# Banded attention: far products that read queries and keys in the tokens' order, with a step of 16 elements

## The reference, cut to what matters

```
OFFSETS = 0..32, 48, 64, 96, 128, 192, 256, 384        # 16 heads of 16 elements
scores[n, delta] = q[n] . k[n - delta] * scale + pos_bias[delta, head]   # -inf where n < delta
out[n] = sum over delta of softmax(scores)[n, delta] * v[n - delta]
x = x + (out * sigmoid(gate)) @ Wout + bout
```

## Time and profile before

| | |
|---|---|
| three runs | 3300.21, 3304.84 and 3306.57 us; median 3304.84 |
| the profiled execution | 3302.18 us; span from first to last instruction 3300.4 us |
| mean granted clock of the span | 0.918 |
| PE, DVE, ACT, POOL busy | 2711.5, 1657.7, 1460.1, 877.2 us |
| banded attention | from the start to about 1330 us |

### The profile page before, as it was taken

How to read it: one execution, slowest core, us unless ns; L and a number is a source line. 1 busy time by engine, 2 the same in 40 slices (tenths; PEclk the granted TensorE clock), 3 DMA queues, 4 the chain that set the end, 5 groups by cost and what they waited for, 6 DMA issues and landing times. The chain is left out here.

```text
span 3300.4 us, 102182 instructions
## 1 busy us (share of the span) xinstructions
PE 2711.5 (82%) x46240; PEld 1581.4 (48%) x46240; DVE 1657.7 (50%) x2797; ACT 1460.1 (44%) x1537; POOL 877.2 (27%) x561
## 2 busy tenths in 40 slices
PE   2678787878787887698669989898989898997897
PEld 1455565656555655443334444444444444443443
DVE  3455444444444444520656666666666666664501
ACT  1344444444444453342225555555555554555522
POOL 3343434343435242000322222222212121211002
PEclk8789888889897988799779999999999999999998
DMA  8333323232433332459132222222212222220498
GB/s 198 81 99 75 96 68 99 66 99 72 105 79 98 75 99 50 124 241 421 61 90 59 59 59 59 59 59 56 61 41 60 50 60 55 59 50 5 173 419 327
DMA packets 232618, 343.72 MB, mean 104 GB/s; under 512 B 113396, under 2 KB 141240, under 8 KB 215800
## 3 DMA queue, kind: packets, MB, share of 16 engines
q1 hardware_dynamic: 206952, 309.35, 32.2%
q10 hardware_dynamic: 25232, 27.83, 3.7%
HBM read 266.02 MB, written 68.71 MB: 101 GB/s over the span
## 5 line engine op out<-in xcount | busy, mean ns | idle before, releaser
L1375 DVE TENSOR_REDUCE b_tops<-b_slot 128x8 f32<-128x1024 f32 x576 | 680.4, 1220 | 335.5 <-PE b_slot L1224 174.1
L1417 ACT ACTIVATE b_probs<-b_slot 128x1024 f32<-128x1024 f32 x576 | 582.6, 1023 | 525.1 <-PE b_slot L1232 369.7
L515 POOL COPY a_q_far<-a_q_near 96x1024 bf16<-96x1024 bf16 x128 | 259.2, 2054 | 293.5 <-PE a_slot L592 216.8
L1174 POOL TENSOR_SCALAR_AFFINE_SELECT b_probs<-b_probs 128x1024 f32<-128x1024 f32 x128 | 139.8, 1093 | 727.7 <-ACT b_probs L1417 727.7
L1252 PE MATMUL b_outT_ps<-b_probs,b_v 128*17 128x128 f32 (+3 forms) x4608 | 317.6, 383 | 6.2 <-ACT b_probs L1417 5.5
L1232 PE MATMUL b_slot<-b_q_stack,b_k_stack 99*128 99x512 bf16 (+3 forms) x1280 | 271.5, 318 | 43.5 <-DVE b_tops L1375 32.1
L901 ACT ACTIVATE a_k_far<-a_k_near 96x1024 bf16<-96x1024 bf16 x128 | 258.3, 2067 | 101.6 <-DMA a_k_near<-parts_near_dram 90.6
L1232 PE MATMUL b_slot<-b_k_stack,b_q_stack 96*128 96x512 bf16 (+3 forms) x1280 | 265.3, 322 | 30.5 <-DVE b_tops L1375 20.1
L864 ACT ACTIVATE a_probs<-a_probs 128x1024 f32<-128x1024 f32 x128 | 133.3, 1053 | 210.1 <-DVE a_probs L795 203.5
L795 DVE TENSOR_TENSOR a_probs<-a_slot,a_bias_k 128x1024 f32<-128x1024 f32 x128 | 154.3, 1218 | 141.9 <-PE a_slot L592 141.5
L804 DVE TENSOR_REDUCE a_tops<-a_slot 128x16 f32<-128x1024 f32 x128 | 156.2, 1222 | 105.9 <-PE a_slot L592 104.8
(11 more groups left out here) (227 smaller groups left out, 4303.3 us busy)
## 6 DMA issues: line engine op xcount, KB each, us to landing
f_w_ring<-in_L_ffn_w_dram SPq DMA_DIRECT2D x128, 1024.0 KB, 17.7
parts_near_dram<-a_parts ACTq DMA_DIRECT2D x96, 256.0 KB
parts_dram<-b_parts SPq DMA_DIRECT2D x96, 256.0 KB
a_k_near<-parts_near_dram SPq DMA_DIRECT2D x128, 128.0 KB, 2.9
b_k_stack<-parts_dram SPq DMA_DIRECT2D x64, 256.0 KB, 6.9
a_q_near<-parts_near_dram SPq DMA_DIRECT2D x64, 192.0 KB, 2.9
b_q_stack<-parts_dram SPq DMA_DIRECT2D x32, 384.0 KB, 4.4
values_dram<-a_v_stage SPq DMA_DIRECT2D x16, 544.0 KB, 4.4
```

The source lines that it names most:

```text
L515: pool.tensor_copy(q_far[far][0:QK_ROWS, h, :].rearrange("p (r a) -> p r a", r=LINKS), q_near[near][0:QK_ROWS, h, :].rearrange("p (a r) -> ...
L1174: pool.affine_select(out=blocks, in_=blocks, compare_op=ALU.is_ge, fill=0.0, base=0, pattern=[[0, NT], [1, P]], channel_multiplier=-1).the ...
L1375: ins = dve.tensor_reduce(out, src, AX.X, ALU.max)
L1417: act.activation(probs_of(b, g, u, h)[:, :], slot_of(step)[:, :], ACT.Exp).then_inc(taken_act, 1)
```

## The change

The far matmuls take their operands from the stacks in the tokens' order: residue r is the slice `r:N:LINKS`, 64 elements that lie 16 elements (32 bytes) apart, both for the weights and for the moving operand. The steps `turn`, the six buffers and their semaphores are gone. PE's `mx` of an even head waits for the stack's loads instead of the two copies. `mt` makes one set of rows with 8 matmuls for 16, DVE copies it without rearranging, ACT has no part in it, and `mrow` issues four DMAs for eight.

```
     first += operands(0) + operands(1) + operands(2) + operands(3)          # was: ... + turned(0) + turned(1)
     first += [("mx", 0, 0, h) for h in range(HG)] + [("fparts", 0, 0)] + projection("q", 0, 1)   # was: ... + turned(2) + ...
-            seq += [...] + [("S", b, g, 1)] + operands(n + 4) + turned(n + 3) + place[1] + top[1]
+            seq += [...] + [("S", b, g, 1)] + operands(n + 4) + place[1] + top[1]
-            seq += ([("fparts",) + after] if more else []) + turned(n + 4) + products + [("ote", b, g)] + place[5]
+            seq += ([("fparts",) + after] if more else []) + products + [("ote", b, g)] + place[5]
...
-        MROW = 16 * HG
+        MROW = 16 * HG // 2
...
         elif kind == "mrow":                       # SP
             sp.wait_ge(taken_dve, count("taken_dve", "mt", b, g))
-            sp.wait_ge(rows_kept, count("mt", "mt", b, g))
             for h in range(HG):
-                for order, rows in enumerate((q_near[...], q_far[...])):
-                    sp.dma_start(rows[QK_ROWS:ALL_ROWS, h % 2, :], neg_rows[order][...]).then_inc(mrows_in[h // 2], 16)
+                sp.dma_start(q_near[...][QK_ROWS:ALL_ROWS, h % 2, :], neg_rows[...]).then_inc(mrows_in[h // 2], 16)
...
-                ins = pe.matmul(dst[...], left[1][rows, h, RES * r:RES * (r + 1)], right[1][rows, h, RES * r:RES * (r + 1)], ...)
+                ins = pe.matmul(dst[...], left[rows, h, r:N:LINKS], right[rows, h, r:N:LINKS], ...)
...
         elif kind == "mx":                         # PE
-            pe.wait_ge(turned_q, turns)
-            pe.wait_ge(turned_k, turns)
+            if h % 2 == 0:
+                n = ring(b, g, h // 2, BY_TOKEN)
+                pe.wait_ge(stacked[n], STACK * count(f"stack{n}", "stack", b, g, h // 2))
...
-            for at, i in [(at, i) for at in (AT_ROWS, 2 * AT_ROWS) for i in range(NT)]:      # mt, PE
+            for i in range(NT):
...
-            ins = dve.tensor_copy(neg_rows[1].rearrange("c (r a) -> c r a", r=LINKS), src[...].rearrange("c (a r) -> c r a", r=LINKS))
+            ins = dve.tensor_copy(neg_rows, src[AT_ROWS:AT_ROWS + HG * PARTS, :])
...
-        elif kind == "mt":                         # ACT
-            act.activation(neg_rows[0], slot_of(step)[AT_ROWS:AT_ROWS + HG * PARTS, :], ACT.Copy).then_inc(rows_kept, 1)
...
-        elif kind == "turn":                       # POOL; on ACT the same with k_far and k_near
-            for h in range(2):
-                pool.tensor_copy(q_far[far][0:QK_ROWS, h, :].rearrange("p (r a) -> p r a", r=LINKS),
-                                 q_near[near][0:QK_ROWS, h, :].rearrange("p (a r) -> p r a", r=LINKS)).then_inc(turned_q, 1)
```

More of the change, by code:

```diff
@@ L176, in band_schedule @@
     first = [("z", 0, 0), ("zt", 0, 0), ("z", 0, 1), ("zt", 0, 1)] + projection("q", 0, 0) + projection("k", 0, 0)
-    first += operands(0) + operands(1) + operands(2) + operands(3) + turned(0) + turned(1)
+    first += operands(0) + operands(1) + operands(2) + operands(3)
     first += [step for i4 in range(2) for step in (("v", 0, i4), ("vout", 0, i4))]
-    first += [("mx", 0, 0, h) for h in range(HG)] + turned(2) + [("fparts", 0, 0)] + projection("q", 0, 1)
+    first += [("mx", 0, 0, h) for h in range(HG)] + [("fparts", 0, 0)] + projection("q", 0, 1)
     first += [("fp", 0, 0), ("mred", 0, 0), ("mt", 0, 0), ("mrow", 0, 0)]
@@ L197, in band_schedule @@
             far = [("PV", b, g, 1, c) for c in range(NT)]
[L198 removed]
+            seq += [("vin", b, g), ("S", b, g, 0)] + place[0] + top[0] + [("S", b, g, 1)] + operands(n + 4) + place[1] + top[1]
             seq += [("S", b, g, 2)] + place[2] + [("S", b, g, 3)] + top[2] + place[3] + top[3]
@@ L271, in band_attention @@
         o_bias = sb("o_bias", [P, D])
-        neg_rows = [row_home[at:at + HG * PARTS, :] for at in (AT_ROWS, 2 * AT_ROWS)]
+        neg_rows = row_home[AT_ROWS:AT_ROWS + HG * PARTS, :]
         ident16 = sb("ident16", [P, P], BF16)
@@ L376, in _ @@
                     pool.wait_ge(ident_made, 5)
-                    for stack in k_near + k_far:
+                    for stack in k_near:
                         pool.memset(stack[QK_ROWS:ALL_ROWS, :, :], 1.0)
@@ L538, in _ @@
                         sp.wait_ge(taken_dve, count("taken_dve", "mt", b, g))
-                        sp.wait_ge(rows_kept, count("mt", "mt", b, g))
                         for h in range(HG):
-                            for order, rows in enumerate((q_near[ring(b, g, h // 2, BY_TOKEN)], q_far[ring(b, g, h // 2, BY_RESIDUE)])):
-                                sp.dma_start(rows[QK_ROWS:ALL_ROWS, h % 2, :], neg_rows[order][PARTS * h:PARTS * (h + 1), :]).then_inc(mrows_in[h // 2], 16)
+                            sp.dma_start(q_near[ring(b, g, h // 2, BY_TOKEN)][QK_ROWS:ALL_ROWS, h % 2, :], neg_rows[PARTS * h:PARTS * (h + 1), :]
+                                         ).then_inc(mrows_in[h // 2], 16)
                     elif kind == "vout":
@@ L586, in products @@
                         at = 64 * i - lo
-                        pe.matmul(dst[BLK * c:BLK * (c + 1), at + first:at + last], left[0][rows, h, BLK * blk:BLK * (blk + 1)],
-                                  right[0][rows, h, first:last], start=start, stop=True, skip_group_check=True)
+                        pe.matmul(dst[BLK * c:BLK * (c + 1), at + first:at + last], left[rows, h, BLK * blk:BLK * (blk + 1)],
+                                  right[rows, h, first:last], start=start, stop=True, skip_group_check=True)
                     for r in range(LINKS):
@@ L591, in products @@
                         at = 512 + 64 * pair
-                        ins = pe.matmul(dst[RES * r2:RES * (r2 + 1), at:at + 64], left[1][rows, h, RES * r:RES * (r + 1)],
-                                        right[1][rows, h, RES * r:RES * (r + 1)], start=start, stop=True, skip_group_check=True)
+                        ins = pe.matmul(dst[RES * r2:RES * (r2 + 1), at:at + 64], left[rows, h, r:N:LINKS],
+                                        right[rows, h, r:N:LINKS], start=start, stop=True, skip_group_check=True)
                     return ins
@@ L613, in stacks @@
                 def stacks(b, g, pair):
-                    near, far = ring(b, g, pair, BY_TOKEN), ring(b, g, pair, BY_RESIDUE)
-                    return (q_near[near], q_far[far]), (k_near[near], k_far[far])
+                    n = ring(b, g, pair, BY_TOKEN)
+                    return q_near[n], k_near[n]
                 for step in seq:
@@ L893, in _ @@
                         store(2, *step[1:])
[L894 to L902, removed]
                     elif kind in BY_ACT:
```

31 lines of the change are left out of this document (6 added, 25 removed).

## The result

| | before | after |
|---|---|---|
| median of the runs, us | 3304.89 (3300.21 to 3306.57) | 3350.93 (3349.12 to 3370.91) |
| ratio, 95% interval | | 1.0154 [1.012, 1.0188] |
| PE, DVE, ACT, POOL busy in the profiled execution | 2711.5, 1657.7, 1460.1, 877.2 | 2920.0, 1664.9, 1177.8, 611.2 |

The kernel became slower: by 46 us between the medians, by 51 us (1.54%) by the ratio. The profiled execution of after is the longest of its runs (3370.91 us), so its trace holds some 20 us more than the median, and only differences well above that are read from it. Of the lines, 592 is now 573 (far matmuls), 587 is 568, 636 is 617 and 655 is 636.

A forecast was written before the change was run, and what follows sets the result against it. PE was taken to set the pace, with its work plus 231 us of standing. Savings of 52 + 36 + 14 + 8 = 110 us less 48 for strided reads gave 62 us less, 3243 us, range 3195 to 3350.

The forecast's parts named there:

- the price of the step: Far matmuls: operands with 32 bytes between columns cost 0.34 us more a product, 48 us on the path.
- the point of decision: Far matmuls: from 0.58 us more a product on, the added cost outweighs the 110 us saved.
- the rival of the f32 price: Far matmuls: a column costs 1.81 ns as at line 1849, 0.50 us a product, 3285 us; chance 0.10.
- The trace has no bf16 read like that: Far matmuls: ground for pricing the step from f32 reads with the same 32 bytes, lines 1849 and 1869, ratio 2.07.
- The weights were taken as hidden: Far matmuls: strided weight loads run beside the matmuls ahead; eight f32 loads took 0.95 us with the step, 1.00 without.
- The reads in turn: Far matmuls: strided weights and columns not read side by side, seven rounds 0.99 us, 3330 us in all; chance 0.26.
- The savings: PE in the stage: waits for copies and zT 52, wait for rows 36, `mt` 14, clock 8; 110 us in all.
- the zT wait: Ahead of the first matmul of `mx`: 17.1 us waiting for ACT's eviction of zT, 12 taken to go.
- the rows: Ahead of `S`: the 49.4 us wait for the DMAs of the maxima was to fall by 36 us.
- The rival of the waits that come back: S/mx parts: PE then waits for DVE, half of the 52 + 8 us stays, 3273 us; chance 0.12.
- The clock: PE after long waits: half speed for 6 us, 1 us regained in each of eight groups, 8 us.
- the prediction's own formula: Far products: eight a group at the step's price, less 1.2 us PE has to spare, over 32 groups.

The follow-up runs named there:

- flat: The changed kernel with the far matmuls reading 64 neighbouring columns for both operands (other tokens than the reference's): 3220.25 us, 0.9777 of before.

## Why the prediction was wrong

**The step that failed is the price of the step.** The prediction had 0.34 us for a far product, from the ratio 2.07 of lines 1849 and 1869. Measured are .93 - .24 = .69 us at full and .93 - .39 = .54 at half clock, some .62 in the mean, beyond the 0.58 us that the prediction gave as the point of decision. A ratio was the wrong form: the read has a time of its own, nearly the same at both clocks, and a narrower type does not shorten it. The trace of before had shown the first half of this. Line 1849 takes as long at a granted clock of 0.50 (1434.16 to 1435.60 us) as at 1.00, while line 1869, here at 0.51 (1574.00 to 1575.40 us), takes nearly twice its time; so the ratio of 2.07 holds at full clock alone:

```profile
1434.16 2.05 PE L1849 MATMUL f_ps<-f_w_ring,f_mergedT 128*32 128x256 f32 x16 [1.24 <-PEq L1573]
...
1574.01 1.94 PE L1869 MATMUL f_ps<-f_w_ring,f_hidT 128*32 128x256 f32 x16 [1.95 <-DMA f_w_ring<-in_L_ffn_w_dram]
```

The columns alone cost .81 us / 448 = 1.81 ns, line 1849's value. So the rival of the f32 price had the size right to the hundredth; what it lacked was the weights. The sum also prices seven rounds where a product has eight: the far matmuls' busy time rose by 185 us / 252 = .73 us a product, for the .34 of the prediction.

**A premise beside it was false.** "The trace has no bf16 read like that" overlooked lines 515 and 901 in the earlier trace rows: the copies that go away read these very stacks with this very step, 2054 and 2068 ns for 1024 elements, 2.0 ns each. Seven rounds at that rate are .90 us. They stood in the sum only as waits that end.

**The weights were taken as hidden.** Alone they hold a round for .86 us / 7 = 123 ns, and the stage's clock falls to .79. The row chosen was of f32 in a transpose of 32 rows; the 32 rows are not the reason that it showed no price. Nor does it compare like with like: the granted clock is 0.50 around the loads with the step (1370.00 to 1371.40 us) and 0.83 around those without (832.50 to 833.80 us), and the matmuls beside them have 32 and 128 columns. Yet .95 us / 1024 columns is .93 ns, half of what the bf16 weights paid.

**The reads in turn** came nearest in the total (3330) by a mechanism that is not there: its 0.99 us assumed 141 ns for two reads one after the other, and the runs show two reads of 116 and 123 ns side by side in 133. The Trainium skill (SBUF — State Buffer, section A bandwidth-pool intuition that's wrong (but worth ruling out)) gives the weights a second, independent read port; .93 us for both, where the sum would be 1.67, agrees.

**The savings** were right wait by wait and too high in the sum. The copies' 46.0 us went, and of the zT wait's 17.1 all instead of 12; the rows gave 38 for 36. `mt` gave 7.7 for 14 (half as many matmuls, 21.9 us for 29.6). But flat, where the price is absent, is only 74 us better, not 110. Its idle time in the stage is 1190 - 998 = 192 us, 60 less than before, where 88 were forecast; its busy time is 18 less, where `mt` and the clock were to give 22. Some of the waits came back, ahead of line 653's products with the values (line 672 before), of line 695's transposes of the result (line 714) and of the far products. Groups of flat, 100 to 1290 us:

```profile
L653 PE MATMUL a_outT_ps<-a_probs,a_v_near 128*17 128x64 f32 x7680 | 154.0, 232 | 22.9 <-ACT a_probs L844 13.8 <-issue 8.9
...
L573 PE MATMUL a_slot<-a_q_near,a_k_near 99*64 99x64 bf16 x2048 | 63.6, 209 | 7.4 <-issue 7.3
...
L573 PE MATMUL a_slot<-a_k_near,a_q_near 96*64 96x64 bf16 x1984 | 61.0, 208 | 7.0 <-issue 7.0
L568 PE MATMUL a_slot<-a_q_near,a_k_near 99*32 99x64 bf16 x3968 | 60.4, 204 | 28.1 <-DMA a_q_near<-a_row_home 10.3 <-DVE a_tops L785 9.8 <-issue 7.9
...
L695 PE MATMUL a_slot<-ident,a_outT 128*128 128x128 f32 x256 | 43.4, 323 | 25.7 <-DVE a_probs L776 15.0 <-ACT a_outT L850 7.2 <-issue 3.6
```

and of before, 100 to 1370 us:

```profile
L672 PE MATMUL a_outT_ps<-a_probs,a_v_near 128*17 128x64 f32 x7680 | 150.8, 230 | 16.6 <-issue 11.0 <-ACT a_probs L864 5.6
...
L714 PE MATMUL a_slot<-ident,a_outT 128*128 128x128 f32 x256 | 50.0, 359 | 13.6 <-DVE a_probs L795 12.5 <-ACT a_outT L877 1.1
```

These three rose by 6, 12 and 12 us. The rival of the waits that come back was so in part true, though DVE, which it named, is little of it: its share ahead of the transposes went from 12.5 to 15.0 us and ahead of `S` from 5.7 to 9.8. ACT has more of it (1.1 to 7.2 ahead of the transposes, 5.6 to 13.8 ahead of the products with the values).

**The clock** was counted as a gain of 8 us; in after it is a loss (.83 for .86), and in flat, without the price, it rises to .88.

**The sum with the measured terms.** By the prediction's own formula, (8 x .62 - 1.2) x 32 = 120 us on the path, less 74: 46 us slower, and 46 is the difference of the medians. That this agrees is luck. By the ratio the loss is 51 us; with all eight rounds of a product (.71 us) the formula gives 143 - 74 = 69 us; and the price as measured (125 us) holds the lower clock as well, which the formula doesn't. In the traces PE is busy for 227 us more in after than in flat, 190 of them in line 573 and 37 in lines that the step does not touch. How much of the 125 us is the clock's is not settled.

## What to carry to other kernels

Before a copy that rearranges is replaced by a strided read, look at what the copy itself pays per element: the reader that took its place here paid about the same (2.08 ns for 2.0), and pays it each time it reads. Take such a price as a time per 16 bytes, not as a ratio to a read without gaps, and look at it at both clocks. And where a strided read can't be avoided, put a few of the elements that it takes side by side; the moving operand can then be read in more than one dimension.

## What the runs showed of the hardware

- A read of SBUF in which each element lies on another 16 bytes took 1.8 to 2.1 ns an element on PE (columns 1.81, weights 1.93, both 2.08), POOL (2.01) and ACT (2.02); with two on 16 bytes 1.02 on PE and 1.04 on POOL. On PE a granted clock of 0.50 changed it little against 1.00: seven rounds took .93 and .93 us with both steps, .86 and .86 with the weights', .84 and .81 with the columns'. Two matmuls ran side by side in each round here, four at line 1849, which paid the same 1.81 ns; one alone was not tried.
- The granted clock of the stage was .93 with strided columns over 96 or 99 rows, .78 with the same rounds over 32 rows (one run), and .79 with strided weights over 96 or 99. PE was busy through most of the stage in all three. What in them brings the clock down was not tried.
- Eight f32 weight loads of 128 columns with 32 bytes between them took .95 us at a granted clock of 0.50, .93 ns a column, and eight without gaps 1.00 at 0.83, where bf16 weights with a step of 32 bytes paid 1.93 ns a column. Why is open.
